# Decoder layer: the feed-forward half as one stage, with 16 bit integers between its parts

## The chip, the cores and the metric

The kernel runs on one core of a Trainium2 chip. The metric is the device time of one execution in microseconds; the time of a kernel is the median of its runs.

## The reference

`x` has 16 sequences of 512 rows of 512 numbers. The first half (attention with a decaying sum, a second scan over the context, two layer norms) gives the rows that the program calls x2. The second half, the one that is changed, is a feed-forward layer with quantized activations and weights, and a last layer norm:

```python
def act_qdq(x):
    scale = jnp.maximum(jnp.max(jnp.abs(x)) / qmax, 1e-12)      # qmax = 32767, one scale for the whole array
    return jnp.clip(jnp.round(x / scale), -qmax - 1.0, qmax) * scale
...
x = act_qdq(x)                                  # (8192, 512)
up = act_qdq(x @ lpbq_dequant(w_up).T)          # (8192, 1536)
gate = act_qdq(x @ lpbq_dequant(w_gate).T)      # (8192, 1536)
sig = fixed_qdq_u16(jax.nn.sigmoid(gate))       # rounded to 16 bit
gate = act_qdq(gate * sig)
o = act_qdq(gate * up)
return o @ lpbq_dequant(w_down).T
```

Each `act_qdq` needs the largest magnitude of its whole array before one element of it can be rounded. So the second half can't run in one pass: s_x, s_u, s_g, s_gs and s_o, the five scales, each close a pass or are found by a shortcut.

## The kernel before

Four engines compute: PE multiplies matrices, DVE and ACT work on tiles of 128 partitions, POOL helps; SP issues DMAs. Every engine runs its own list in the order in which it is written, and waits for the others by counting semaphores. There is no scheduler: the code's order is the engine's order. NB = 16 steps (sequences); T = 512 columns.

A number with 16 bits is multiplied as a sum of two parts, high and low (qh and ql, later oh and ol), with weights that are split in the same way, so one product of 128 x 128 by 128 x 512 takes three matmuls: high by high, low by high weights, high by low weights. A "tile" below is 12 matmuls (four slices of 128 rows, three each) into one PSUM bank; a "chunk" is four tiles, 128 x 2048.

*up_gate_phase.* For each step PE makes 24 tiles, up and gate chunks in turn, into six banks. ACT takes each tile out to `group` (L951) and applies silu to gate chunks (L958). DVE finds maxima of each chunk (L1001, L1004, L1005), and the maximum of silu(gate)·up by chunk (L1008, L1011). SP stores every chunk as 32 bit numbers (L909). The x2 rows of the next step are rounded by DVE (L988), turned by PE in four groups of four transposes (L1054; two groups behind tile 11, two behind tile 13), and split by ACT (L941) and DVE (L993):

```python
if g == 2 and nxt:
    high(b + 1, 1 - par)     # ACT, behind the eviction of tiles 8 to 11
...
if g == 3 and nxt:
    low(b + 1, 1 - par)      # DVE, ahead of the maxima of tiles 12 to 15
```

*scales_phase.* From the maxima s_u and s_g follow. s_gs is taken from the largest gate alone, when silu of it is over 0.28. For s_o only the two chunks with the largest maxima are read again, if the third largest is below the first by more than a margin; otherwise all 48 chunks are passed through twice. The flag `go_through` says which (L1299), and every engine reads it.

*down_phase.* Each chunk of gate and up is read again and goes through POOL (rounding gate and up, L1485, L1490, with a tiny operation ahead of it, L1484), ACT (sigmoid L1515, rounding L1519 and L1524, high part L1531) and DVE (L1558 rounds the sigmoid, L1560 gate by sigmoid, L1566 by up, L1570 the low part). PE multiplies a chunk by the down weights with 48 matmuls (L1616 to L1618). DVE adds the x2 rows (L1578), takes moments (L1581) and `row_moments`, POOL the root (L1494), ACT scales (L1536) and stores. `step` of DVE takes the begin of one chunk, the middle of the one before and the finish of the one before that.

## Time and profile before

| | us |
|---|---|
| median of 3 runs | 3091.08 |
| runs | 3089.62 to 3091.11 |
| span of the profiled execution | 3087.7 |
| median less span | 3.4 |
| first matmul of up_gate_phase | 1294.47 |
| last matmul of up_gate_phase starts | 2369.45 |
| first matmul of down_phase | 2460.56 |
| last matmul of down_phase starts | 3075.71 |

The span runs from the first to the last instruction of the profiled execution; the profile gives no other time of that execution, so the 3.4 us between the median and the span stand for what lies around the span. Matmul records overlap: a record lasts 0.39 us, while the next one starts 0.23 us later. So PE's pace is read from starts.

### The profile page before, as it was taken

How to read it: one execution, taken by the hardware profiler on the slowest of the kernel's cores; microseconds unless marked ns; L12 is line 12 of the kernel's file. 1: busy time of each engine (PE TensorE's matmuls, PEld its weight loads, DVE VectorE, ACT ScalarE, POOL GpSimd, SP SyncE). 2: the span in 40 equal slices, each digit the busy share in tenths (PEclk: the TensorE clock that was granted, in tenths of full speed). 3: DMA queues.
4: the chain of work that ended last, by engine and by line, in shares of the span. 5: the costliest groups of instructions: out<-in, count | busy, mean ns of one | idle time of the engine just before them, and what ended most of it. 6: DMA issues, size and time to landing. Idle time of an engine off the chain costs nothing. (4 is left out here: it accounts for less than half of the span.)

```text
span 3087.7 us, 32437 instructions
## 1 busy us (share of the span) xinstructions
PE 2757.5 (89%) x12272; PEld 2261.6 (73%) x12272; DVE 2280.7 (74%) x2242; ACT 1327.2 (43%) x1396; POOL 588.0 (19%) x266
## 2 busy tenths in 40 slices
PE   2589999999999999599999999999997198988988
PEld 2477777777777777488888888888885177777776
DVE  8678988889888998565555555555555688888886
ACT  2233433444333433243333333333333466666664
POOL 4111111112111111000000000000000485555552
PEclk7789999999999999899999999999998599999999
DMA  6211111111111111332222322222223555555552
GB/s 238 96 41 62 68 54 54 68 60 69 54 54 63 66 54 42 124 140 104 109 109 109 122 109 109 109 102 104 107 109 135 207 205 216 217 217 217 216 206 82
DMA packets 58129, 357.18 MB, mean 116 GB/s; under 512 B 6496, under 2 KB 6496, under 8 KB 17248
## 3 DMA queue, kind: packets, MB, share of 16 engines
q1 hardware_dynamic: 54480, 330.33, 28.5%
q10 hardware_dynamic: 3600, 26.22, 2.1%
q8 instruction: 29, 0.48, 0.1%
q14 instruction: 20, 0.16, 0.0%
HBM read 212.87 MB, written 143.65 MB: 115 GB/s over the span
## 5 line engine op out<-in xcount | busy, mean ns | idle before, releaser
L1062 PE MATMUL ug_out<-ug_qh,ug_wh 128*128 128x512 f32 x1536 | 601.3, 391 | 2.8 <-DVE ug_ql L993 1.4
L1064 PE MATMUL ug_out<-ug_qh,ug_wl 128*128 128x512 f32 x1536 | 598.5, 390 | 0.0
L1063 PE MATMUL ug_out<-ug_ql,ug_wh 128*128 128x512 f32 x1536 | 598.1, 389 | 0.0
L951 ACT ACTIVATE ug_group<-ug_out,scales 128x512 f32<-128x512 f32 x384 | 263.2, 690 | 607.3 <-PE ug_out L1064 604.5
L1616 PE MATMUL dn_ps<-down_wh,dn_oh 128*128 128x512 f32 x768 | 314.4, 409 | 148.3 <-DVE dn_ol L1570 148.3
L1004 DVE TENSOR_REDUCE ug_step_max<-ug_group 128x1 f32<-128x2048 f32 x48 | 109.7, 2285 | 335.4 <-ACT ug_group L951 335.4
L1062 PEld LDWEIGHTS ug_out<-ug_qh,ug_wh 128*128 128x128 f32 x1536 | 288.8, 188 | 62.6 <-DVE ug_wl L1016 2.0
L1064 PEld LDWEIGHTS ug_out<-ug_qh,ug_wl 128*128 128x128 f32 x1536 | 288.6, 188 | 60.5
L1063 PEld LDWEIGHTS ug_out<-ug_ql,ug_wh 128*128 128x128 f32 x1536 | 288.9, 188 | 59.0
L1617 PE MATMUL dn_ps<-down_wl,dn_oh 128*128 128x512 f32 x768 | 310.6, 404 | 0.0
L1618 PE MATMUL dn_ps<-down_wh,dn_ol 128*128 128x512 f32 x768 | 310.2, 404 | 0.0
L1616 PEld LDWEIGHTS dn_ps<-down_wh,dn_oh 128*128 128x128 f32 x768 | 151.8, 198 | 187.3 <-DVE dn_ol L1570 155.1
L717 PE MATMUL qk_ps<-xh,wah 128*128 128x512 f32 x512 | 201.4, 393 | 26.8 <-DVE xl L531 26.8
L1198 POOL MEMSET sc_magic<- 128x1 f32 x1 | 0.1, 99 | 1094.0 <-POOLq L849 1094.0
L718 PE MATMUL qk_ps<-xl,wah 128*128 128x512 f32 x512 | 200.7, 392 | 0.0
L721 PE MATMUL qk_ps<-xh,wal 128*128 128x512 f32 x512 | 200.6, 392 | 0.0
L449 ACT ACTIVATE phi<-qk_ps 128x1024 f32<-128x1024 f32 x64 | 65.9, 1029 | 263.6 <-PE qk_ps L721 263.6
L1001 DVE TENSOR_REDUCE ug_step_max<-ug_group 128x1 f32<-128x2048 f32 x48 | 109.7, 2286 | 90.3 <-ACT ug_group L951 90.3
L1617 PEld LDWEIGHTS dn_ps<-down_wl,dn_oh 128*128 128x128 f32 x768 | 152.3, 198 | 32.2
L1618 PEld LDWEIGHTS dn_ps<-down_wh,dn_ol 128*128 128x128 f32 x768 | 151.4, 197 | 33.0
L1485 POOL TENSOR_SCALAR dn_gate<-dn_gate,scales 128x2048 f32<-128x2048 f32 x48 | 168.6, 3512 | 0.0
L1515 ACT ACTIVATE dn_gs<-dn_gate,scales 128x2048 f32<-128x2048 int16 x48 | 96.6, 2013 | 152.3 <-POOL dn_gate L1485 152.3
(211 smaller groups left out, 5712.6 us busy)
## 6 DMA issues: line engine op xcount, KB each, us to landing
up_products<-ug_group SPq DMA_DIRECT2D x48, 1024.0 KB, 3.9
gate_products<-ug_group SPq DMA_DIRECT2D x48, 1024.0 KB, 3.9
dn_gate<-gate_products SPq DMA_DIRECT2D x48, 1024.0 KB, 4.9
dn_up<-up_products SPq DMA_DIRECT2D x48, 1024.0 KB, 4.8
xt_raw<-in_xT SPq DMA_DIRECT2D x64, 256.0 KB, 2.8
csq<-in_ctx_rows SPq DMA_DIRECT2D x16, 1024.0 KB, 6.7
xrow<-in_x_rows SPq DMA_DIRECT2D x16, 1024.0 KB, 4.8
x_rows<-xrow SPq DMA_DIRECT2D x16, 1024.0 KB, 3.9
```

Of the source, the lines that this page charges most:

```text
L717: pe.matmul(out, sh, mh, start=(k == 0), stop=False)
L718: pe.matmul(out, sh, ml, start=False, stop=False)
L721: mm = pe.matmul(out, sl_, mh, start=False, stop=(k == n - 1))
L951: act.activation(group[:, n % 4, m * T:(m + 1) * T], out_ps[(g * GM + m) % 6][:], ACT.Copy, scale=s_x).then_inc(evacuated, 1)
L1001: dve.tensor_reduce(step_max[:, 0, q:q + 1], part, AX.X, ALU.max, apply_absolute_value=True).then_inc(step_max_ready, 1)
L1062: pe.matmul(o, wh[:, m, k], qh[:, par, k], start=(k == 0), stop=False)
L1063: pe.matmul(o, wh[:, m, k], ql[:, par, k], start=False, stop=False)
L1064: mm = pe.matmul(o, wl[:, m, k], qh[:, par, k], start=False, stop=(k == KC - 1))
L1485: pool.tensor_scalar(gate[:, n], gate[:, n], inv_g, MAGIC, ALU.mult, ALU.add).then_inc(g_round, 1)
L1616: pe.matmul(o, oh[:, n, k, rows], mh, start=(n == 0 and k == 0), stop=False)
L1617: pe.matmul(o, oh[:, n, k, rows], ml, start=False, stop=False)
L1618: mm = pe.matmul(o, ol[:, n, k, rows], mh, start=False, stop=(n == NC3 - 1 and k == KC - 1))
```

## The change

The three phases become one, `ffn_phase`, in one block without barriers inside it. It has three stages. The gate stage makes all gate tiles (12 a step) and stores them as 32 bit numbers, together with the rounded and turned x2 as 16 bit integers. The up stage reads those integers again (no turning), makes all up tiles, and beside them finishes gate chunks: ACT rounds a stored gate chunk to int16 (`gate_chunk_16`) and takes its sigmoid, POOL rounds that to uint16 (`round_sigmoid`), DVE multiplies both and rounds to int16 (`gated`), and SP stores the result. DVE multiplies gs by up for the maxima by tile (192 cells in place of 48 chunks). The down stage reads up as 32 bit and gs as 16 bit numbers; POOL rounds up, DVE makes the rounded product in one instruction (`product`) and the low part, ACT the high part. The weights of one of the three matrices are in SBUF at a time, so they are split again at the start of each stage. Inside the up stage DVE runs `low` of the next step at the head of its round for the third chunk.

```diff
-def up_gate_phase(nc, x2_dram, w_ffn_t, up_dram, gate_dram, amax_x2, acc, rmax, scales):
...
+def ffn_phase(nc, x2_dram, w_ffn_t, q_dram, up_dram, gate_dram, gs_dram, amax_x2, out):
...
+        x2 = raw
+        up16, o16, x2_res = g16, sr16, group
+        banks = [ctx.enter_context(nc.psum_tensor(f"ff_ps{i}", [P, T], F32)) for i in range(8)]
+        turn_ps, out_ps = banks[0:2], banks[2:8]
...
+                def up_step(b, par, ahead):
+                    if ahead:
+                        load_q(b + 1, 1 - par, 16 * (NB // 2))
+                    for g in range(NG):
+                        t = NG * b + g
+                        if ahead:
+                            sp.wait_ge(sr_ready, t + 1)
+                            load_gate(b + 1, g)
+                        sp.wait_ge(gs_ready, t + 1)
+                        sp.dma_start(gs_dram[b, g], gs16[:, g]).then_inc(gs_stored[g], 16)
+                        sp.wait_ge(evacuated, GM * (NG * (NB + b) + g + 1))
+                        sp.dma_start(up_dram[t], group[:, g]).then_inc(stored[g], 16)
...
+                def round_sigmoid(b, par, g, first=False):
+                    t = NG * b + g
+                    pool.wait_ge(sig_ready, t + 1)
+                    if not (first and g < 2):
+                        pool.wait_ge(gs_ready, t - 1)
+                    wait(pool, tick_done, t)
+                    pool.tensor_tensor(tick[:], mhalf[:, 0:1], mhalf[:, 0:1], ALU.mult).then_inc(tick_done, 1)
+                    pool.tensor_scalar(sr16[:, (NG * par + g) % 2], raw[:, g], 65536.0, 0.0, ALU.mult, ALU.add).then_inc(sr_ready, 1)
+
+                def up_step(b, par, ahead):
+                    for g in range(NG):
+                        if g < NG - 1:
+                            round_sigmoid(b, par, g + 1, isinstance(b, int) and b == 0)
+                        elif ahead:
+                            round_sigmoid(b + 1, 1 - par, 0)
...
+                def quantize(b, par):
+                    for c in range(KC):
+                        act.wait_ge(turned, KC * b + c + 1)
+                        if c == 0 and not (isinstance(b, int) and b < 2):
+                            act.wait_ge(q_stored[par], 16 * (b // 2) if isinstance(b, int) else 16 * ((b - par) >> 1))
+                        act.activation(q16[:, par, c], turn_ps[c % 2][:], ACT.Copy, scale=inv_x).then_inc(q_ready, 1)
+                        act.wait_ge(q_ready, KC * b + c + 1)
+                        act.activation(hi[:, par, c], q16[:, par, c], ACT.Copy).then_inc(hi_ready, 1)
...
+                def gate_step(b, par, ahead, first=False):
+                    for g in range(NG):
+                        if not first:
+                            act.wait_ge(stored[g], 16 * b)
+                            act.wait_ge(gate_max_ready, 2 * (NG * (b - 1) + g) + 2)
+                        evacuate(b, par, g, range(GM))
+                        if first and g < NG - 1:
+                            weights_high(g + 1)
+                        if g == 1 and ahead:
+                            quantize(b + 1, 1 - par)
...
+                        evacuate(NB + b, par, g, (0, 1))
+                        if more:
+                            gate_chunk_16(nb, npar, ng, first and ng > 0)
+                        evacuate(NB + b, par, g, (2,))
+                        if more:
+                            gate_chunk_sigmoid(nb, npar, ng)
+                        evacuate(NB + b, par, g, (3,))
+                        if first and g < NG - 1:
+                            weights_high(NG + g + 1)
+                        if not ahead:
+                            weights_high(2 * NG + g)
+                        if g == 1 and ahead:
+                            high(b + 1, 1 - par)
...
+                def low(s, par):
+                    for c in range(KC):
+                        dve.wait_ge(hi_ready, KC * s + c + 1)
+                        dve.tensor_tensor(lo[:, par, c], q16[:, par, c], hi[:, par, c].bitcast(F32),
+                                          ALU.subtract).then_inc(lo_ready, 1)
+
+                def gate_step(b, par, ahead, first=False):
+                    for g in range(NG):
+                        t = NG * b + g
+                        if g == 2 and ahead:
+                            low(b + 1, 1 - par)
+                        if first and g > 0:
+                            weights_low(g)
+                        dve.wait_ge(evacuated, GM * (t + 1))
+                        dve.tensor_reduce(gate_max[:, 0, bass.ds(t, 1)], group[:, g], AX.X, ALU.max).then_inc(gate_max_ready, 1)
+                        dve.tensor_reduce(gate_max[:, 1, bass.ds(t, 1)], group[:, g], AX.X, ALU.min, negate=True).then_inc(gate_max_ready, 1)
+
+                def gated(b, par, g):
+                    t = NG * b + g
+                    sl = (NG * par + g) % 2
+                    dve.wait_ge(sr_ready, t + 1)
+                    if not (isinstance(b, int) and b == 0):
+                        dve.wait_ge(gs_stored[g], 16 * b)
+                    dve.scalar_tensor_tensor(gs16[:, g], sr16[:, sl], gs_factor, g16[:, sl], ALU.mult, ALU.mult).then_inc(gs_ready, 1)
+
+                def up_step(b, par, ahead, first=False):
+                    for g in range(NG):
+                        t = NG * b + g
+                        nb, npar, ng = (b, par, g + 1) if g < NG - 1 else (b + 1, 1 - par, 0)
+                        if g == 2 and ahead:
+                            low(NB + b + 1, 1 - par)
+                        if first and g > 0:
+                            weights_low(NG + g)
+                        dve.wait_ge(evacuated, GM * (NG * (NB + b) + g + 1))
+                        dve.tensor_reduce(up_max[:, bass.ds(t, 1)], group[:, g], AX.X, ALU.max,
+                                          apply_absolute_value=True).then_inc(up_max_ready, 1)
+                        dve.wait_ge(gs_ready, t + 1)
+                        dve.tensor_tensor(prod[:, 0], gs16[:, g], group[:, g], ALU.mult).then_inc(prod_ready, 1)
+                        dve.wait_ge(prod_ready, t + 1)
+                        dve.tensor_reduce(cell_max[:, bass.ds(GM * t, GM)], prod[:, 0].rearrange("p (m t) -> p m t", t=T), AX.X,
+                                          ALU.max, apply_absolute_value=True).then_inc(cell_ready, 1)
+                        if g < NG - 1 or ahead:
+                            gated(nb, npar, ng)
+                        if not ahead and g < NG - 1:
...
+                weights_low(NG)
+                low(NB, 0)
+                dve.wait_ge(gate_top_known, 1)
...
+                dve.wait_ge(cell_ready, NCH)
+                dve.tensor_copy(packed[:, 1:], cell_max[:]).then_inc(packed_ready, 1)
...
+                def product(b, par, g):
+                    t = NG * b + g
+                    sl = (NG * par + g) % 2
...
+                    dve.scalar_tensor_tensor(o16[:, sl].bitcast(I16), gs16[:, g], o_factor, up16[:, sl],
+                                             ALU.mult, ALU.mult).then_inc(o16_ready, 1)
...
+                def down_step(b, par, k=None, bias=True, ahead=True):
+
+                    product(b, par, 1)
+                    ol_chunk(b, par, 0)
+                    if k is not None and bias:
+                        norm_bias(b - 2)
+                    product(b, par, 2)
+                    ol_chunk(b, par, 1)
+                    if k is not None:
+                        sums(b - 1, 1 - par, k)
+                    if ahead:
+                        product(b + 1, 1 - par, 0)
+                    ol_chunk(b, par, 2)
...
+                def turn(b, par, tiles):
+                    pe.wait_ge(x2_in[par], 16 * (b // 2 + 1) if isinstance(b, int) else 16 * ((b - par) >> 1) + 16)
+                    for c in tiles:
+                        wait(pe, q_ready, KC * b + c - 1)
+                        for j in range(TT):
+                            mm = pe.transpose(turn_ps[c % 2][:, j * P:(j + 1) * P],
+                                              x2[:, par, j * HID + c * P:j * HID + (c + 1) * P], ident[:])
+                        mm.then_inc(turned, 1)
+
+                def tile(s, par, m, first):
+                    if not (first and m < 6):
+                        pe.wait_ge(evacuated, MT * s + m - 5)
+                    for k in range(KC):
+                        o = out_ps[m % 6][:]
+                        pe.matmul(o, wh[:, m, k], hi[:, par, k], start=(k == 0), stop=False)
+                        pe.matmul(o, wh[:, m, k], lo[:, par, k], start=False, stop=False)
+                        mm = pe.matmul(o, wl[:, m, k], hi[:, par, k], start=False, stop=(k == KC - 1))
+                    mm.then_inc(out_ready, 1)
+
+                def step(s, par, turn_next=False, weights=None, first=False):
+                    pe.wait_ge(lo_ready, KC * (s + 1))
+                    for m in range(MT):
+                        if weights is not None and m % GM == 0:
+                            pe.wait_ge(wl_ready, weights + m // GM + 1)
+                        tile(s, par, m, first)
+                        if m == 5 and turn_next:
+                            turn(s + 1, 1 - par, (0, 1))
+                        if m == 7 and turn_next:
+                            turn(s + 1, 1 - par, (2, 3))
...
```

ACT's list in a step of the gate stage. Before, in up_gate_phase, behind tile 11 of a step (ug_out are the PSUM banks of tiles, ug_turn those of turned x2):

```order
L951 ACTIVATE ug_group<-ug_out4,scales 128x512
L951 ACTIVATE ug_group<-ug_out5,scales 128x512
L941 ACTIVATE ug_qh<-ug_turn0 128x512
L941 ACTIVATE ug_qh<-ug_turn1 128x512
L941 ACTIVATE ug_qh<-ug_turn0 128x512
L941 ACTIVATE ug_qh<-ug_turn1 128x512
L951 ACTIVATE ug_group<-ug_out0,scales 128x512
```

The same place of the change, behind tile 7 (ff_ps2 and ff_ps3 hold tiles 6 and 7, ff_ps0 and ff_ps1 the turned x2):

```order
L1201 ACTIVATE ff_group<-ff_ps2,ff_scales 128x512
L1201 ACTIVATE ff_group<-ff_ps3,ff_scales 128x512
L1188 ACTIVATE ff_q16<-ff_ps0,ff_scales 128x512
L1190 ACTIVATE ff_hi<-ff_q16 128x512
L1188 ACTIVATE ff_q16<-ff_ps1,ff_scales 128x512
L1190 ACTIVATE ff_hi<-ff_q16 128x512
L1188 ACTIVATE ff_q16<-ff_ps0,ff_scales 128x512
L1190 ACTIVATE ff_hi<-ff_q16 128x512
L1188 ACTIVATE ff_q16<-ff_ps1,ff_scales 128x512
L1190 ACTIVATE ff_hi<-ff_q16 128x512
L1201 ACTIVATE ff_group<-ff_ps4,ff_scales 128x512
```

Each group of turned columns now takes two instructions, the second of which waits for the first, and PE's third and fourth group of transposes, which are behind tile 7 in its list, wait for the first and the second L1188.

DVE's list in a step of the up stage, in the loop, between the second and the third chunk of a step (ff_lo is the low part of the next step's x2, ISA and REGISTER_ALU are waits and their arithmetic):

```order
L1377 TENSOR_REDUCE ff_cell_max<-ff_prod 128x4
L1358 REGISTER_ALU
L1361 SCALAR_TENSOR_TENSOR ff_gs16<-ff_sr16,ff_scales,ff_g16 128x2048
L1340 ISA
L1341 TENSOR_TENSOR ff_lo<-ff_q16,ff_hi 128x512
L1340 REGISTER_ALU
L1341 TENSOR_TENSOR ff_lo<-ff_q16,ff_hi 128x512
L1340 REGISTER_ALU
L1341 TENSOR_TENSOR ff_lo<-ff_q16,ff_hi 128x512
L1340 REGISTER_ALU
L1341 TENSOR_TENSOR ff_lo<-ff_q16,ff_hi 128x512
L1371 ISA
```

Before, the same subtraction (L993) was in the middle of a step of 24 tiles, with 12 tiles to go; now it is behind the four operations of the second chunk, in a step of 12 tiles. In up_gate_phase DVE's list there was:

```order
L1001 TENSOR_REDUCE ug_step_max<-ug_group 128x1
L992 ISA
L993 TENSOR_TENSOR ug_ql<-ug_turn0,ug_qh 128x512
L992 REGISTER_ALU
L993 TENSOR_TENSOR ug_ql<-ug_turn1,ug_qh 128x512
L992 REGISTER_ALU
L993 TENSOR_TENSOR ug_ql<-ug_turn0,ug_qh 128x512
L992 REGISTER_ALU
L993 TENSOR_TENSOR ug_ql<-ug_turn1,ug_qh 128x512
L999 ISA
L1004 TENSOR_REDUCE ug_step_max<-ug_group 128x1
```

The two lists differ in what is ahead of the subtractions (one reduction, against two reductions and two operations on 2048 columns for each chunk) and in their first operand, which is in SBUF now and was in PSUM before.

## Rows read from the trace of the kernel before

**Rows 1.** The page, the granted clock in 40 slices of the span.

```profile
PEclk7789999999999999899999999999998599999999
```

**Rows 2.** Windows of the profile: length, busy time and count by engine, PEclk, DMA share, GB/s.

```profile
1294.50:2370.20 1075.70, 1073.95 (x4848) 890.71 (x4848) 598.19 (x331) 391.55 (x497) 0.00 (x0) 1.00 0.28 111
...
2460.50:3076.50 616.00, 557.93 (x2304) 453.86 (x2304) 524.13 (x401) 404.00 (x242) 340.61 (x148) 0.94 0.55 201
```

**Rows 3.** Timeline of PE: start, duration, and idle time before it in brackets.

```profile
1294.47 0.79 PE L1062 MATMUL ug_out<-ug_qh,ug_wh 128*128 128x512 f32 x1 [1.41 <-DVE ug_ql L993]
...
2369.45 0.39 PE L1064 MATMUL ug_out<-ug_qh,ug_wl 128*128 128x512 f32 x1
...
2460.56 0.80 PE L1616 MATMUL dn_ps<-down_wh,dn_oh 128*128 128x512 f32 x1 [90.72 <-DVE dn_ol L1570]
...
3069.82 0.39 PE L1616 MATMUL dn_ps<-down_wh,dn_oh 128*128 128x512 f32 x1
...
3075.71 0.39 PE L1618 MATMUL dn_ps<-down_wh,dn_ol 128*128 128x512 f32 x1
```

**Rows 4.** Groups by line from 1150 us on: busy us, mean ns, idle before.

```profile
L1485 POOL TENSOR_SCALAR dn_gate<-dn_gate,scales 128x2048 f32<-128x2048 f32 x48 | 168.6, 3512 | 0.0
...
L1570 DVE TENSOR_TENSOR dn_ol<-dn_up,dn_oh 128x2048 fp32r<-128x2048 int16 x48 | 130.2, 2713 | 3.4 <-ACT dn_oh L1531 3.4
...
L1515 ACT ACTIVATE dn_gs<-dn_gate,scales 128x2048 f32<-128x2048 int16 x48 | 96.6, 2013 | 152.3 <-POOL dn_gate L1485 152.3
...
L1578 DVE SCALAR_TENSOR_TENSOR dn_x<-dn_ps,scales,dn_x 128x512 f32<-128x512 f32 x64 | 47.1, 736 | 17.0 <-PE dn_ps L1618 17.0
```

**Rows 5.** Timeline of ACT and DVE at the end of a chunk, in the loop.

```profile
1801.03 1.08 ACT L941 ACTIVATE ug_qh<-ug_turn 128x512 fp32r<-128x512 int16 x2
...
1813.14 0.69 ACT L951 ACTIVATE ug_group<-ug_out,scales 128x512 f32<-128x512 f32 x1 [2.03 <-PE ug_out L1064]
...
1813.86 2.29 DVE L1004 TENSOR_REDUCE ug_step_max<-ug_group 128x1 f32<-128x2048 f32 x1 [4.72 <-ACT ug_group L951]
...
1818.26 2.28 DVE L1008 TENSOR_TENSOR ug_silu<-ug_silu,ug_group 128x2048 f32<-128x2048 f32 x1
...
1820.67 2.29 DVE L1011 TENSOR_REDUCE rmax<-ug_silu 128x2048 f32 x1
```

**Rows 6.** Timeline of PE at a set of transposes.

```profile
2209.18 1.04 PE L1054 MATMUL ug_turn<-ug_ident,ug_x 128*128 128x128 f32 x8
...
2209.97 0.47 PE L1062 MATMUL ug_out<-ug_qh,ug_wh 128*128 128x512 f32 x1
```

**Rows 7.** Timeline of DVE, four subtractions back to back.

```profile
1240.59 2.49 DVE L646 TENSOR_TENSOR al<-att,ah 128x512 fp32r<-128x512 f32 x4
```

**Rows 8.** Timeline of PE: three restarts after idle time.

```profile
608.98 0.50 PE L717 MATMUL mix_ps<-ah,wah 128*128 128x512 f32 x1 [1.42 <-DVE att L612]
...
2640.89 0.50 PE L1616 MATMUL dn_ps<-down_wh,dn_oh 128*128 128x512 f32 x1 [3.12 <-DVE dn_ol L1570]
...
2679.95 0.80 PE L1616 MATMUL dn_ps<-down_wh,dn_oh 128*128 128x512 f32 x1 [4.52 <-DVE dn_ol L1570]
```

**Rows 9.** Timeline of POOL and DVE: the scan with and without POOL, a rounding alone.

```profile
1043.14 5.17 POOL L421 TENSOR_TENSOR csq_l<-csq,csq_h 128x2048 fp32r<-128x2048 f32 x1 [19.15 <-ACT csq_h L480]
...
1043.76 5.63 DVE L551 TENSOR_TENSOR_SCAN kv<-decay,kv 128x512 f32<-128x512 f32 x1
...
1053.62 1.21 DVE L551 TENSOR_TENSOR_SCAN kv<-decay,kv 128x512 f32<-128x512 f32 x1
...
2747.67 1.99 POOL L1490 TENSOR_SCALAR dn_up<-dn_up,scales 128x2048 f32<-128x2048 f32 x1
```

**Rows 10.** A DVE operation of three operands from SBUF: count, min/median/max ns.

```profile
L617 DVE SCALAR_TENSOR_TENSOR att<-att,v_sb x64: 656/692/694, 194.4 to 1240.0; 128x512 f32<-128x512 f32 x64
```

**Rows 11.** Timeline of the decision in the second stage, and SP's first load behind it.

```profile
2384.66 0.15 DVE L1299 CAST sc_go_through<-sc_tmp 128x1 int32<-128x1 f32 x1
...
2387.46 0.36 SPq L1175 DMA_DIRECT2D sc_gate<-gate_products  x1
```

1118 lines of the change are left out of this document (501 added, 617 removed).

## The prediction

> **What bounds the kernel now.** I read the page first, then windows by stage, then PE's timeline at the seams, and last the groups by line. The page's clock row shows the granted clock at its upper level of 2.4 GHz except at the start and at two places, slice 17 (1235 to 1312 us) and slices 31 and 32 (2316 to 2470) [rows 1]: these are the seams between phases. The windows say what is between them. While up and gate tiles are made PE is busy all the time, 1073.95 of 1075.70 us, with DVE at 598 and ACT at 392: that stage is PE's [rows 2]. Then PE stands still for 90.7 us, while the scales are found and the down stage fills [rows 2, 3]. In the down stage DVE is busy for 524 of 616 us and PE has gaps; it runs 16 steps in 615 us, 39 us a step on average [rows 2, 3]. PE's own pace: 26 matmuls apart are 3069.82 and 3075.71, 0.2266 us each [rows 3], so a step of 144 matmuls is 32.63 us, and the down stage has 16 x 6 us to give. The first half, up to 1294.47, is not touched.
>
> **The change part by part.** The sum is made against the profiled span, 3087.7 us; the median of the runs is 3.4 us above it, and I add those back.
>
> *Products.* 4608 matmuls at 0.2266 are 1044.2 us; the window of 1075.7 less this leaves 31.5 us for 15 sets of turning, 2.1 each. The change makes the same matmuls and as many transposes (they don't turn again in the up stage). Nothing is gained or lost here, if PE never waits. It now waits at four kinds of places.
>
> *Gate stage, turning.* PE's third group of transposes, behind tile 7, waits for the first L1188, and ACT has that one behind the eviction of tile 7. Count from the end E of tile 7: eviction E+0.04, next ACT instruction 0.58 later (the spacing of L951, and L941 pairs of 0.60 in 1.08), 0.69 long, so E+1.31; PE's third group at E+1.4. The second L1188 is behind L1190, which waits for its own engine: it ends near E+2.5, PE's fourth group starts at E+2.6 [rows 5]. Half a set takes 0.4 us, so the next tile starts at E+3.05; before, a whole set of eight took 0.79 and the next tile started 0.6 behind E [rows 6]. Loss 2.4 us a step, in 14 steps: **+34**. From below this could be 1.5 a step (both groups wait for one instruction only), from above 2.4 + 1.75 where the clock falls too. It shouldn't: the gaps are 1.3 and 0.7 us, and after 1.42 us of idle the first matmul lasted 0.50, not the 0.80 of a restart at 1.2 GHz [rows 8].
>
> *First gate step.* The low weights of tiles 4 to 7 and 8 to 11 are made by DVE behind the two maxima of the chunk ahead. From a chunk's end: 0.7 for the eviction, 4.5 for two reductions of 2.29, 2.2 for the subtraction: PE waits 7.6 us for the second chunk. For the third there are four subtractions of the next x2 as well (2.5 us, [rows 7]): 9.7. After idle time PE starts at the lower clock. The price of that: 2640.89 to 2679.95 are 39.06 us, of which 4.52 idle and 32.8 work, which leaves 1.75 us, after an idle time of 3.12 [rows 8]; I take 2.2 behind longer ones. Together **+22**. The start itself is 1.5 us earlier, since x2 is turned before the scale is known: **-1.5**.
>
> *Gate to up.* Behind the last gate tile: eviction 0.7, two maxima 4.5, two tiny ones, low weights 2.2, four subtractions 2.4: PE waits 10.4 us. Its next four tiles end near 23; their chunk's maximum, product, cell maxima and `gated` (2.29 each, 8.9 in all, [rows 5]) stand ahead of the next low weights: 12.2 more. For the third chunk the same and four subtractions: 14.5. With three restarts of 2.2: **+44**. Before, this seam did not exist.
>
> *Up stage, steady.* DVE has 3 x 8.9 + 2.5 = 29.3 us of work in a step of 32.63, ACT 23, POOL 6 to 11, by 2.0 us for a rounding alone and its mean of 3.5 where DVE's operations stand in its way [rows 4, 9]. So PE should set the pace, but the order is tight. Count from S, PE's first matmul of a step. Tile 7 ends at S+21.9, its eviction at S+22.7, DVE starts the maximum 0.03 later [rows 5]. Then 2.2 (next), 2.2 and 0.2 for the wait on its own result (1818.26 to 1820.67 is 2.41), 2.2, 2.2: the subtractions start at S+31.7, 0.60 apart, and the last ends at S+34.2 [rows 5, 7]. PE wants it at S+32.63. Loss 1.6 us a step, and at such an idle time the clock stays. It holds for 14 steps (the first up step has its successor ready early): **+22**.
>
> *Up to down.* Behind the last up tile: eviction 0.7, maximum, product and cell maxima 6.8, the reduction over partitions of 193 columns 1.3, some ten small DVE operations 2: the flag at 11. SP's first load came 2.8 us behind the flag [rows 11]; I estimate that two pairs of small loads land at 18, then ACT 1.1, DVE 2.4, the last low weights 2.3, the scale 1, POOL's first rounding 2 to 4, and `product` 2.3 twice, low part 2.3: PE starts 35 us behind its last tile, where it was 90.7 [rows 3]: **-56**. Bounds: 28 with every load ahead, 50 if the loads or POOL's rounding wait for each other.
>
> *Down stage.* DVE: three times `product` and low part, 4.6 us (the low part's mean of 2.71 has POOL's interference in it), and the sums, 4 x 1.4 + 0.8: 20 us of 32.63. ACT: 3 x 2.0 + 3. POOL 6.5 to 12 [rows 4]. The low part of the third chunk is ready some 4 us ahead of its use. Loads of the next step wait for the store of two steps before and land, by my estimate, 8 us into the step; `product` wants them at 10.5. So PE sets the pace: 16 x 32.63 + 2 against 615.4: **-91**. From above +30 if those loads are late by 2 us in each step. The tail is unchanged.
>
> Sum: 34 + 22 - 1.5 + 44 + 22 - 56 - 91 = -26.5. 3087.7 - 26.5 + 3.4 = 3064.6; I forecast **3065 us**.
>
> *A rule against it.* `gated` is a scalar_tensor_tensor with both tensors in SBUF, and neither is bfloat16. The nearest row is L617, 692 ns for 512 columns, what any two-input operation takes [rows 10]; so I price 2048 columns at 2.29. The Trainium skill, Vector Engine (DVE) Microarchitecture Reference, section "Points that are easy to get wrong", says that such an instruction runs at half rate. This case's trace disagrees, with 692 ns; by the rule it would be 1.3 us for 512 columns, and the total is that of the last rival below.
>
> **The rivals.**
>
> *POOL takes DVE's place in the up stage (slower).* ACT's sigmoid of the next step's first chunk starts at S+30.7 and lasts 2.01 [rows 4], so POOL's small operation comes at S+32.8 to 32.9 and its rounding 0.2 later, while DVE is in its four subtractions (S+31.7 to 34.2). The rows of the first half show who wins. POOL's L421 came at 1043.14 behind a DVE operation; the scan that DVE had next lasted 5.63 in place of 1.21: POOL got in at the boundary, and DVE stood still until it was through [rows 9]. Here a rounding that gets in ahead of the fourth subtraction holds it for the 2.0 us that it lasts alone [rows 9]. PE then waits 3.5 us, and at 3.12 to 3.5 the clock falls (1.75, above): 5.2 a step in place of 1.6, 14 x 3.6 = 51 more, 3065 + 51 = **3115**. It turns on 0.1 us: POOL's small operation must be there before the third subtraction starts, at S+32.9. Each DVE operation that is a little longer than I take it (an integer operand, a scale from SBUF) speaks for it, each wait of ACT or POOL against it. Which instructions wait for POOL can't be read off before, where only DVE operations with two SBUF inputs did; the maxima aren't among them, I take them as free. Chance 0.30. The GPSIMD Engine Reference of the Trainium skill, section "Specifications", names the same two engines' shared SBUF interfaces; the trace agrees, with those 5.63 us.
>
> *The down stage doesn't get PE's pace.* If the late loads or POOL hold the third chunk, 37 us a step, +70: 3135 with the rest as forecast; at 34 a step it is +22, 3087. Against it: DVE's and ACT's load halves. Chance 0.10.
>
> *The change doesn't shorten the search for s_o.* If the condition for all chunks held, 96 passes over a chunk of some 10 us each: over 4000. The reference's numbers for these inputs give 42500 for the largest cell and 38719 for the third, against a margin of 4.9. Chance below 0.01.
>
> *Waits that I price are hidden.* If DVE's chain is 1 us shorter and the seams half as long: -45 more, **3020**. Chance 0.08.
>
> *`gated` at half rate.* DVE then has 35.7 us in a step, PE waits 3.7 and restarts slowly: 14 x 3.8 = 53 more, 3118, and some 35 on top where POOL also gets in. By L617 chance 0.05.
>
> **How the numbers follow.** My own case has 0.46; its range is 3045 to 3085 (10 either way at both long seams, 0.9 a step in turning). The range of 3040 to 3125 takes in POOL's rival, which may also hold in only some of the steps. Slower by over 0.2% (6 us, what a measurement of this kernel can tell): POOL's rival in most steps, half the down rival, half rate, a little of my case's errors: 0.32. Within: 0.08. Faster: 0.60.
>
> **What the new profile would show.** PE's idle time ahead of the third and fourth group of transposes, 0.7 to 1.3 us, 15 times. The first matmul of an up step waiting for DVE's last subtraction, 1.5 us (right) or 3.5 with a slow restart (POOL's rival; then that subtraction lasts 2.6 us and not 0.68). PE's longest idle time near 35 us. Down steps of 32.7 us with the clock at 1.00. Wrong it would be by a wait that I read as slack: ACT's evictions behind its two long operations, or loads in the down stage.

## The result, and the profile after

The changed kernel takes 3137.0 us (median of 4 runs, 3136.1 to 3137.9) against 3091.1 us of the kernel before beside it (3089.6 to 3091.6). The ratio is 1.0148, with a 95% interval of 1.0134 to 1.0163: slower by 46 us. The forecast was 3065 us, faster, with a range of 3040 to 3125. It was wrong in sign, and the time lies outside the range.

The profiled execution has a span of 3136.0 us, 48.3 us more than before. First the page's row of the granted clock, which answers to [rows 1].

```profile
PEclk7689999999999999799999998899999978999999
```

Then the windows by stage of the changed kernel: first half, gate stage, the seam with 110 of the first up step's 144 matmuls, the rest of the up stage, the wait between up and down, the down stage, the tail. Columns are as in [rows 2].

```profile
0.00:1294.92 1294.92, 1128.23 (x5121) 918.78 (x5121) 1093.09 (x1441) 483.74 (x633) 217.75 (x99) 0.95 0.20 74
1294.92:1911.41 616.49, 573.08 (x2544) 468.07 (x2544) 251.09 (x156) 211.67 (x318) 0.00 (x0) 0.97 0.32 123
1911.41:1980.00 68.59, 31.79 (x110) 25.04 (x111) 38.23 (x35) 24.80 (x23) 8.48 (x7) 0.70 0.47 184
1980.00:2553.19 573.19, 526.02 (x2196) 428.14 (x2194) 465.38 (x238) 328.62 (x331) 100.72 (x90) 0.95 0.57 216
2553.19:2599.17 45.98, 0.00 (x1) 0.03 (x1) 24.07 (x27) 7.56 (x5) 12.07 (x9) 0.53 0.68 251
2599.17:3123.98 524.81, 524.81 (x2304) 433.98 (x2304) 317.52 (x309) 132.31 (x106) 191.84 (x106) 1.00 0.48 191
3123.98:3136.00 12.02, 0.00 (x1) 0.00 (x0) 2.24 (x8) 2.93 (x4) 1.01 (x1) 0.60 0.21 87
```

The down stage is what the change promised: PE is busy for all of 524.81 us at clock 1.00, where the same 2304 matmuls had 615.44 us before. What eats this, and more, lies in the two product stages. Before, they were one window of 1075.7 us with PE busy throughout [rows 2]. Now they are three, of 616.49 + 68.59 + 573.19 = 1258.27 us, and in none of them is PE always busy. PE's timeline says where it stands; these rows are its restarts (the first matmul behind an idle time), and the bracket is the idle time ahead of each.

```profile
1316.05 0.80 PE L1577 MATMUL ff_ps<-ff_hi,ff_wh 128*128 128x512 f32 x1 [7.49 <-DVE ff_wl L1335]
...
1340.74 0.79 PE L1577 MATMUL ff_ps<-ff_hi,ff_wh 128*128 128x512 f32 x1 [4.95 <-DVE ff_wl L1335]
...
1921.65 0.80 PE L1577 MATMUL ff_ps<-ff_hi,ff_wh 128*128 128x512 f32 x1 [10.24 <-DVE ff_lo L1341]
...
1946.36 0.79 PE L1577 MATMUL ff_ps<-ff_hi,ff_wh 128*128 128x512 f32 x1 [12.08 <-DVE ff_wl L1335]
...
1974.72 0.79 PE L1577 MATMUL ff_ps<-ff_hi,ff_wh 128*128 128x512 f32 x1 [14.49 <-DVE ff_wl L1335]
...
2176.60 0.49 PE L1577 MATMUL ff_ps<-ff_hi,ff_wh 128*128 128x512 f32 x1 [3.37 <-DVE ff_lo L1341]
...
2599.17 0.77 PE L1617 MATMUL ff_ps<-ff_wh,ff_hi 128*128 128x512 f32 x1 [45.98 <-DVE ff_lo L1511]
```

The row at 2176.60 stands for 14 alike, one at each up step from the third on, all of 3.37 us. In the gate stage the transposes wait twice a step, 1.36 and 0.58 us in 12 of its 15 sets (1.45 and 0.52 in two, 3.25 and 0.52 in the first).

The same numbers as a balance against the kernel before, where 2304 matmuls at 0.2266 us are 522.1 us and the 15 sets of turning 31.5 us:

| part | forecast | measured | from |
|---|---|---|---|
| start of the second half | -1.5 | +0.5 | 1294.92 against 1294.47 |
| gate stage: turning and first step | 34 + 22 = 56 | +62.9 | 616.49 - 522.1 - 31.5 |
| gate to up, and up steps | 44 + 22 = 66 | +119.7 | 68.59 + 573.19 - 522.1 |
| up to down | -56 | -44.7 | 45.98 against 90.72 |
| down stage | -91 | -90.6 | 524.81 against 615.44 |
| sum | -26.5 | +47.8 | |

The rest to 48.3 is the tail and rounding. The up part alone is 54 us off. Split further: the three waits at the seam are 36.8 us, with 7.1 us of matmuls at the lower clock, 43.9 together (44 was forecast). So the 14 steady steps lose 75.8 us in place of 22: 47.2 of idle time and 28.6 of matmuls that follow each other more slowly behind it, for the most part at the lower clock (e1 shows how much).

What happens at one of these 14 is in the timelines of DVE and POOL.

```profile
2172.28 4.18 DVE L1341 TENSOR_TENSOR ff_lo<-ff_q,ff_hi 128x512 fp32r<-128x512 int16 x4
...
2174.09 2.37 DVE L1341 TENSOR_TENSOR ff_lo<-ff_q,ff_hi 128x512 fp32r<-128x512 int16 x1
...
2173.36 0.27 POOL L1121 TENSOR_TENSOR ff_tick<-ff_mhalf 128x1 f32<-128x1 f32 x1 [8.96 <-ACT ff_raw L1225]
2173.59 2.34 POOL L1122 TENSOR_SCALAR ff_sr<-ff_raw 128x2048 uint16<-128x2048 f32 x1
```

The first DVE row is the group of four subtractions; the second shows its last one alone. It starts at 2174.09, lasts 2.37 us where its sisters last 0.68, and ends 0.5 us behind POOL's rounding, which began at 2173.59, 0.1 us after the third had started. That looks like the collision that the first half showed with the scan [rows 9]. But an overlap is only an overlap: DVE's chain was late by itself too. The experiments take the two apart.

### The profile page after: what moved, and what is told of

Read it like the earlier page. It is cut to its first block, busy times and chain, and to the rows that moved or that the text cites. A ratio compares the mean times of both kernels' runs of the same rounds, so it can differ in the third digit from the quotient of the medians.

```text
span 3136.0 us, 33437 instructions
## 1 busy us (share of the span) xinstructions
PE 2783.9 (89%) x12272; PEld 2274.0 (73%) x12272; DVE 2191.6 (70%) x2213; ACT 1191.6 (38%) x1420; POOL 531.9 (17%) x311
## 3 DMA queue, kind: packets, MB, share of 16 engines
q1 hardware_dynamic: 72912, 394.04, 32.9%
## 4 chain that ended last, share of the span: by engine, by line
PE 46%; DVE 8%; issue 3%; ACT 2%; POOL 0%; DVEq 0%; POOLq 0%; ACTq 0%
PE ff_ps L1577 10%; PE ff_ps L1578 10%; PE ff_ps L1579 10%; PE ff_ps L1617 5%; PE ff_ps L1618 5%; PE ff_ps L1619 5%; DVE ff_lo L1341 2%; DVE ff_up_max L1372 1%; DVE ff_gs L1361 1%; DVE ff_prod L1375 1%; PE ff_ps L1568 1%; ACT ff_q L1188 1%; DVE ff_wl L1335 0%; ACT ff_group L1201 0%; DVE ff_cell_max L1377 0%
## 5 line engine op out<-in xcount | busy, mean ns | idle before, releaser
L1577 PE MATMUL ff_ps<-ff_hi,ff_wh 128*128 128x512 f32 x1536 | 622.7, 405 | 99.2 <-DVE ff_lo L1341 60.2
L1578 PE MATMUL ff_ps<-ff_lo,ff_wh 128*128 128x512 f32 x1536 | 615.3, 401 | 0.0
L1579 PE MATMUL ff_ps<-ff_hi,ff_wl 128*128 128x512 f32 x1536 | 613.8, 400 | 0.0
L1201 ACT ACTIVATE ff_group<-ff_ps,ff_scales 128x512 f32<-128x512 f32 x384 | 264.8, 690 | 683.2 <-PE ff_ps L1579 670.2
L1577 PEld LDWEIGHTS ff_ps<-ff_hi,ff_wh 128*128 128x128 f32 x1536 | 299.9, 195 | 170.2 <-issue 53.0
L1579 PEld LDWEIGHTS ff_ps<-ff_hi,ff_wl 128*128 128x128 f32 x1536 | 298.9, 195 | 64.7
L1578 PEld LDWEIGHTS ff_ps<-ff_lo,ff_wh 128*128 128x128 f32 x1536 | 300.3, 195 | 62.1
L1617 PE MATMUL ff_ps<-ff_wh,ff_hi 128*128 128x512 f32 x768 | 299.9, 390 | 46.0 <-DVE ff_lo L1511 46.0
L1618 PE MATMUL ff_ps<-ff_wl,ff_hi 128*128 128x512 f32 x768 | 299.7, 390 | 0.0
L1619 PE MATMUL ff_ps<-ff_wh,ff_lo 128*128 128x512 f32 x768 | 299.5, 390 | 0.0
```

The costliest lines, as they stand in the source:

```text
L1201: act.activation(group[:, g, m * T:(m + 1) * T], out_ps[(GM * g + m) % 6][:], ACT.Copy, scale=s_x).then_inc(evacuated, 1)
L1577: pe.matmul(o, wh[:, m, k], hi[:, par, k], start=(k == 0), stop=False)
L1578: pe.matmul(o, wh[:, m, k], lo[:, par, k], start=False, stop=False)
L1579: mm = pe.matmul(o, wl[:, m, k], hi[:, par, k], start=False, stop=(k == KC - 1))
L1617: pe.matmul(o, hi[:, sl, k, rows], mh, start=(g == 0 and k == 0), stop=False)
L1618: pe.matmul(o, hi[:, sl, k, rows], ml, start=False, stop=False)
```

## The experiments

Two theories of the 46 us stood against each other. **Collision**: POOL's rounding takes the place of the last subtraction, and PE's wait grows beyond what the clock bears. **Order**: DVE's chain of long operations is simply too long ahead of the subtractions, and POOL only runs beside it. Seven kernels were run, each made from the changed kernel; e6 and e7 carry several of the changes. Added lines shift line numbers by up to six. The code shown is an excerpt of each change; ... stands for lines left out.

**e1, POOL waits.** POOL's rounding for the next step stays behind the four subtractions; no work moves on DVE.

```
                         elif ahead:
+                            pool.wait_ge(lo_ready, KC * (NB + b + 2))
                             round_sigmoid(b + 1, 1 - par, 0)
```

> In the up stage POOL's rounding of the next step's first sigmoid chunk waits until DVE's four subtractions are through; nothing else is changed. Theory A (POOL gets in ahead of the fourth subtraction and holds DVE): the four subtractions last 2.5 us in place of 4.18, PE's first matmul of an up step waits 1.6 us in place of 3.37, 14 times, which is 25 us. Whether the clock still falls at 1.6 us is open: if it stays, another 26 us come back (75.8 of the steady stage less 47.2 idle is 28.6) and the kernel takes 3086 us; if it falls as before, 3112 us. Theory B (the wait is DVE's own chain of three 2048-column operations a chunk, which are longer than priced, and POOL only runs beside it): the wait stays 3.37 us and the time 3137 us.

Measured: 3088.8 us (10 runs, 3086.4 to 3091.5), 48 us below the changed kernel and level with the kernel before (ratio 0.999, 0.9981 to 1.0). One step of e1, in the timelines of DVE, POOL and PE:

```profile
2156.70 2.49 DVE L1342 TENSOR_TENSOR ff_lo<-ff_q,ff_hi 128x512 fp32r<-128x512 int16 x4
...
2159.67 1.90 POOL L1122 TENSOR_SCALAR ff_sr<-ff_raw 128x2048 uint16<-128x2048 f32 x1
...
2159.33 0.49 PE L1578 MATMUL ff_ps<-ff_hi,ff_wh 128*128 128x512 f32 x1 [1.68 <-DVE ff_lo L1342]
2159.66 0.40 PE L1579 MATMUL ff_ps<-ff_lo,ff_wh 128*128 128x512 f32 x1
```

The four subtractions last 2.49 us, the wait is 1.68 us at all 14 steps, and steps are 34.60 us apart in place of 37.6 to 39.2. The window over them shows the second half of the gain:

```profile
1984.65:2470.72 486.07, 462.58 (x2025) 378.68 (x2024) 413.48 (x225) 305.77 (x310) 86.16 (x84) 1.00 0.66 246
```

PE's clock is 1.00 there (0.95 in the changed kernel). Of the 48 us, 14 x 1.69 = 24 are idle time and the other 24 are the clock. A step is still 34.60 us, 32.63 of work, 1.68 of waiting and 0.29 at the restart, so some 4 of the 28.6 us above belong to the restarts even at the upper clock. The expectation of theory A was 3086 us. The collision theory is shown, with its size, by one wait that takes POOL away and nothing else. What DVE's order costs by itself is the 1.68 us of waiting that stay: close to the 1.6 of the forecast.

**e2, low parts early.** The other way to the same end: POOL is left alone, and DVE makes the subtractions two operations earlier.

```
-                        if g == 2 and ahead:
-                            low(NB + b + 1, 1 - par)
...
                         dve.tensor_tensor(prod[:, 0], gs16[:, g], group[:, g], ALU.mult).then_inc(prod_ready, 1)
+                        if g == 1 and ahead:
+                            low(NB + b + 1, 1 - par)
```

> In the up stage the four subtractions of the next step's integers move ahead in DVE's order by two operations: behind the product of the second chunk, ahead of its cell maxima and of the next gate chunk's product. No work is removed and POOL's instructions are as they were. They would end 4.6 us earlier in the step, 3 us ahead of PE's need, and POOL's rounding would meet other DVE operations that nothing waits for. Theories A (POOL's hold) and B (DVE's own chain) both give no wait at the start of an up step, 47 us of idle and 28 us of slow clock back: 3061 us, up steps of 32.7 us. Theory C (DVE, ACT and POOL are too full for a step of 32.63 us, so that the wait comes back in another place, at the evictions or the products): 3100 us or more.

Measured: 3061.7 us (3059.3 to 3063.5), ratio to the kernel before 0.9904 (0.9887 to 0.992). 75 us come back, the 75.8 that the steady steps lost. The up steps of e2 in one window:

```profile
1983.60:2476.19 492.59, 492.59 (x2174) 407.54 (x2172) 440.42 (x238) 325.63 (x329) 108.28 (x90) 1.00 0.67 251
```

PE has no idle time in 492.59 us, with DVE at 440. So DVE was never too full for the stage; moving four operations up in its list is enough, with POOL's list as it was. Theory C, that the wait would come back elsewhere, falls. This run can't tell collision from order, since both expected its result; e1 does that. POOL's rounding now meets other operations, and one such place is instructive:

```profile
2181.41 2.34 DVE L1361 SCALAR_TENSOR_TENSOR ff_gs<-ff_sr,ff_scales,ff_g 128x2048 int16<-128x2048 uint16 x1
...
2182.55 1.25 POOL L1121 TENSOR_TENSOR ff_tick<-ff_mhalf 128x1 f32<-128x1 f32 x1 [8.97 <-ACT ff_raw L1225]
```

Here POOL's small operation came in the middle of a long DVE operation, and it was POOL that stood still: 1.25 us in place of 0.19 (e1), until DVE's 2.34 us were over. POOL's rounding then ran from 2183.77 on beside the maximum, which has one input and was not held:

```profile
2183.67 2.28 DVE L1370 TENSOR_REDUCE ff_up_max<-ff_group 128x2048 f32 x1
```

**e3, turning split.** ACT takes the first two turned tiles between the evictions of tiles 5 and 6.

```
-                        evacuate(b, par, g, range(GM))
+                        if g == 1 and ahead:
+                            evacuate(b, par, g, (0, 1))
+                            quantize(b + 1, 1 - par, (0, 1))
+                            evacuate(b, par, g, (2, 3))
+                            quantize(b + 1, 1 - par, (2, 3))
+                        else:
+                            evacuate(b, par, g, range(GM))
...
-                        if g == 1 and ahead:
-                            quantize(b + 1, 1 - par)
```

> In the gate stage ACT takes the first two turned tiles between the evictions of tiles 5 and 6 and the last two behind that of tile 7, so that PE's third and fourth group of transposes find their banks free. The two waits of 1.36 and 0.58 us go in 14 steps (27 us), and 3.8 us in the first step. Theory A (the clock falls in every other gate step because of these two small gaps; such steps last 38.4 us against 36.8): another 11 us, together 3095 us, gate steps of 34.7 us. Theory B (the transposes themselves lower the clock, as they show 0.63 us for four): the 11 us stay, 3106 us.

Measured: 3092.5 us (10 runs, 3090.3 to 3094.4), 44.5 us below the changed kernel, ratio to the kernel before 1.0003 (0.9994 to 1.0013). The gate stage of e3:

```profile
1293.00:1866.81 573.81, 557.29 (x2544) 462.15 (x2544) 250.97 (x156) 211.68 (x318) 0.00 (x0) 0.98 0.34 132
```

It lasts 573.81 us against 616.49. Of the 42.7 us, 26.9 are idle time (43.4 less the 16.5 that remain in the first step) and 15.8 are matmuls at the lower clock and transposes that are no longer cut in two. The time is 2.5 us below theory A's: with the same transposes and no gaps the clock stays at 1.00 from 1377 to 1860 us, where the changed kernel has 0.98, so theory B falls. Small gaps cost the clock as well, and the two of 1.36 and 0.58 us, with four transposes between them, did lower it, though 1.68 us alone in e1 did not. In the first step nothing was gained: the 3.25 us wait went, and the wait for low weights behind it grew from 4.95 to 9.02 us.

**e4, seams.** Low weights ahead of the maxima, high weights ahead of the evictions, and all three groups of up weights during and just behind the last gate step. This is DVE's part; ACT's high weights and SP's loads of weights move with it.

```
-                        if first and g > 0:
-                            weights_low(g)
+                        if first and g < NG - 1:
+                            weights_low(g + 1)
                         dve.wait_ge(evacuated, GM * (t + 1))
...
+                        if not ahead and g < 2:
+                            weights_low(NG + g)
+                            if g == 1:
+                                low(NB, 0)
...
-                        if first and g > 0:
-                            weights_low(NG + g)
...
-                weights_low(NG)
-                low(NB, 0)
+                weights_low(NG + 2)
```

> Low weights come ahead of the maxima in DVE's order and high weights ahead of the evictions in ACT's at both places where weights change: in the first gate step, and between gate and up, where all three groups of up weights and the first subtractions are made while the last gate step runs and just behind it. If DVE's order is all that makes these five waits (7.49 and 4.95; 10.24, 12.08 and 14.49 us), they go with their restarts at the slow clock: 36.8 + 7.1 at the seam, some 12.4 + 4 in the first gate step, 60 us together, 3077 us. Rival: the transfers of the weights (a buffer for two of them) or the search for the gate scale, which ACT and POOL wait for with all evictions behind it, take their place: half of it at most, 3105 us.

Measured: 3090.2 us (10 runs, 3086.8 to 3093.2), 47 us below the changed kernel, between the two expectations. All five waits for weights are gone, and one new wait stands at the second up step. In the timeline of PE, and behind it of POOL and DVE:

```profile
1938.37 0.80 PE L1579 MATMUL ff_ps<-ff_hi,ff_wh 128*128 128x512 f32 x1 [12.49 <-DVE ff_lo L1342]
...
1898.93 2.32 POOL L1114 PARTITION_ALL_REDUCE ff_gate_top_all<-ff_gate_top  x1 [611.32 <-DVE ff_gate_top L1401]
1911.73 0.18 POOL L1122 TENSOR_TENSOR ff_tick<-ff_mhalf 128x1 f32<-128x1 f32 x1 [10.48 <-issue]
...
1913.91 4.05 DVE L1366 SCALAR_TENSOR_TENSOR ff_gs<-ff_sr,ff_scales,ff_g 128x2048 int16<-128x2048 uint16 x1 [10.34 <-POOL ff_sr L1123]
```

PE now goes through the first up step without a stop, but `gated` for the first chunk can't be made until the gate scale is known and POOL has rounded. DVE begins its chunks of 9.0 us at 1913.9, and the subtractions of the second step stand behind them. The wait moved from the weights to the scale; 12.5 us of idle and a restart are the price. Of POOL's 10.48 us, the last 4.5 are behind the sigmoid that it needed (ready at 1907.2): POOL was not ready itself.

**e5, rounding first.** This looks at up to down, where the wait was 46 us and not 35. In the changed kernel:

```profile
2577.07 2.31 POOL L1160 PARTITION_ALL_REDUCE ff_amax_o<-ff_amax_o  x1 [11.36 <-DVE ff_amax_o L1488]
2588.17 0.18 POOL L1152 TENSOR_TENSOR ff_tick<-ff_mhalf 128x1 f32<-128x1 f32 x1 [8.79 <-issue]
...
2590.45 4.11 DVE L1505 SCALAR_TENSOR_TENSOR ff_sr<-ff_gs,ff_scales,ff_g 128x2048 int16<-128x2048 int16 x1 [10.10 <-POOL ff_g L1153]
```

The scale was known at 2580.3, and DVE then waited 10.1 us for POOL, which stood still for 8.8 us behind its reduction and waited for no other engine.

```
+                round_up(0, 0, 0, True)
+                round_up(0, 0, 1, True)
                 pool.wait_ge(o_max_part, 1)
                 pool.partition_all_reduce(amax_o[:], amax_o[:], P, bass.bass_isa.ReduceOp.max).then_inc(o_reduced, 1)
-                round_up(0, 0, 0, True)
-                round_up(0, 0, 1, True)
                 round_up(0, 0, 2, True)
```

> Between up and down POOL rounds the first two chunks of up products ahead of its reduction over partitions of the largest product, and not behind it; their data and scale are there by then. In the changed kernel POOL's first small operation starts 8.8 us behind the end of that reduction though nothing it needs is late. Theory A (POOL needs these 9 us for its first ordinary operation behind any such reduction): with the roundings ahead of it they are done when the scale s_o is known, DVE's first product starts at once behind the scale instead of 10.1 us later, and PE's wait between up and down falls from 46 to 36 to 38 us, a gain of 8 to 10 us, 3128 us. Theory B (POOL waits for something that the trace does not name, such as the loads of up products): its roundings start at the same time as before, the reduction itself is delayed behind them, and the kernel gains nothing or loses some us.

Measured: 3130.0 us (3129.8 to 3130.5), 7 us below the changed kernel; its ratio to the kernel before is 1.0121 (1.0104 to 1.0138). PE's wait is 39.8 us, 6.1 less. The timeline of POOL in e5:

```profile
2571.55 0.18 POOL L1152 TENSOR_TENSOR ff_tick<-ff_mhalf 128x1 f32<-128x1 f32 x1 [7.14 <-issue]
2571.73 1.96 POOL L1153 TENSOR_SCALAR ff_g<-ff_raw,ff_scales 128x2048 int16<-128x2048 f32 x1
...
2583.36 0.38 POOL L1162 PARTITION_ALL_REDUCE ff_amax_o<-ff_amax_o  x1 [6.59 <-issue]
2593.45 0.18 POOL L1152 TENSOR_TENSOR ff_tick<-ff_mhalf 128x1 f32<-128x1 f32 x1 [9.72 <-issue]
```

DVE's first product follows the scale at once, as theory A said. But POOL paid at the other side too: the reduction, whose input was there at 2576.0, started only at 2583.36, 6.6 us behind POOL's last rounding, and the next rounding 9.7 us behind the reduction. The wait of 7.14 us in the first row comes on top: a memset, at 2564.31, lies between it and the reduction before. The timeline leaves out one kind of row that names what all these pauses have in common. The views of single lines have it (changed kernel, then e5):

```profile
L1138 POOLq MODIFY_POOL_CONFIG  x2: 6/6/6, 2545.6 to 2545.6; - x2
L1152 POOLq MODIFY_POOL_CONFIG  x2: 83/83/83, 2579.3 to 2579.4; - x2
...
L1152 POOLq MODIFY_POOL_CONFIG  x4: 11/46/83, 2564.4 to 2583.7; - x4
L1162 POOLq MODIFY_POOL_CONFIG  x2: 8/8/8, 2577.0 to 2577.0; - x2
```

In every run a pair of these small instructions stands on POOL's queue at the start of each of these pauses, in both directions. Where POOL goes on at once, as from the first reduction to the `affine_select` behind it at 1287.44, there is none, nor ahead of the memset that comes 2.9 us behind a reduction. Where POOL had to wait anyway the pause is hidden: the pair of L1138 stands at 2545.6, right behind the last rounding, and its reduction starts at 2561.78, 0.1 us behind its input. In e5 the pair of L1162 makes the pause ahead of the reduction: the scale is known 8.7 us behind the reduction's input, where it took 3.4 in the changed kernel. These 5.3 us are why PE's wait fell by 6.1 us and not by the 10.1 of DVE's. What POOL does between the pair and the next operation the rows don't say. The Trainium skill, GPSIMD Engine Reference, section "Instruction dispatch", says that the first call to freshly loaded code costs about 6 us, with nothing visible in the profile for that time, and measures it from the instruction of this name. That fits; the pauses with nothing else to wait for are 6.0 (e6) to 10.1 us here, and no run took the change of code away.

**e6, together**: e2, e3, e4 and e5.

> The edits of e2, e3, e4 and e5 together. From 3137 us e2 took 75, e3 took 44.5 and e4 took 47. If their waits are independent and e5 takes 9, the time is 2961 us. The 12.5 us wait that e4 left at the second up step shrinks with e2's order by two operations, 4.5 us, so 2957 us. Rival: an up stage that starts with ACT and DVE behind (the evictions of the first up step queue behind the search for the gate scale) does not catch up when PE no longer pauses at each step, and waits come back step by step: 2990 us or more.

Measured: 2958.4 us (2956.1 to 2959.4), ratio to the kernel before 0.9564 (0.9548 to 0.958). The four gains of 75, 44.5, 47 and 7 us add up to 173.5, and 178.6 came: they are all but independent. Of the 5 us more, 2.2 are the wait at the second up step, which is now 10.25 us, and another 2.3 lie in the first gate step, where e3 alone had gained nothing because the low weights came late. In the windows of e6 (gate stage with the first up step; the other 15 up steps; down stage) PE is all but never idle:

```profile
1294.12:1878.63 584.51, 584.50 (x2688) 485.79 (x2688) 277.90 (x183) 235.19 (x342) 8.47 (x7) 1.00 0.38 146
1878.63:2380.38 501.75, 491.50 (x2160) 406.66 (x2160) 455.00 (x247) 328.32 (x331) 109.33 (x90) 0.99 0.67 254
2419.70:2944.63 524.93, 524.93 (x2304) 434.23 (x2304) 318.59 (x309) 132.31 (x106) 190.25 (x107) 1.00 0.48 192
```

What is left beside PE's own work in the second half is one wait of 10.25 us at the second up step and one of 39.3 us between up and down.

**e7, low parts first.** e6, with the high parts and the subtractions of the second up step behind the first chunk. One condition changes in two places, ahead of `low` in DVE's list and ahead of `high` in ACT's:

```
-                        if g == 1 and ahead:
+                        if g == (0 if first else 1) and ahead:
                             low(NB + b + 1, 1 - par)
```

It also builds the identity for the transposes ahead of POOL's first reduction and not behind it.

> e6, and in the first up step ACT makes the high part and DVE the subtractions of the next step's integers behind the first chunk in place of the second. Theory A (PE's wait at the second up step is only for these subtractions, which stand behind four chunks of 8.9 us that began late): that wait goes, 8 us and a slow restart of 2 us below e6, 2947 us. Theory B (the four chunks themselves are late, so PE then waits for the evictions of the second up step): no gain over e6.

Measured: 2957.4 us (2956.4 to 2959.0), the same as e6. PE's waits, in its timeline:

```profile
1881.00 0.50 PE L1583 MATMUL ff_ps<-ff_hi,ff_wh 128*128 128x512 f32 x1 [0.49 <-DVE ff_lo L1346]
...
1921.05 0.79 PE L1583 MATMUL ff_ps<-ff_hi,ff_wh 128*128 128x512 f32 x1 [7.12 <-DVE ff_lo L1346]
```

The wait at the second step fell from 10.25 to 0.49 us, and a new one of 7.12 us stands at the third. So theory A is refuted in what matters: DVE is behind by its chunks, and with 29 us of work in a step of 32.6 it needs more than a step to catch up. From the first product to the last up tile e7 takes 1.7 us less than e6, not 10. The expectation names e6 and one edit; the identity was a second one. POOL's timeline, and behind it PE's last matmul of the first half in e6 and in e7:

```profile
1278.69 0.29 POOL L1110 TENSOR_SCALAR_AFFINE_SELECT ff_ident<-ff_ident 128x128 f32<-128x128 f32 x1 [0.15 <-POOL ff_mhalf L1108]
1289.09 0.38 POOL L1112 PARTITION_ALL_REDUCE amax_x<-amax_x  x1 [10.11 <-issue]
...
1258.01 0.47 PE L717 MATMUL mix_ps<-csq_h,strip_h 128*128 128x512 f32 x1 [0.88 <-DVE xrow L660]
...
1259.27 0.47 PE L717 MATMUL mix_ps<-csq_h,strip_h 128*128 128x512 f32 x1 [0.87 <-DVE xrow L660]
```

PE turned x2 four microseconds earlier than in e6, but POOL's reduction, and with it the scale, came later: the first product starts at 1295.73 us, 1.6 later than in e6 (1294.12). Of these, 1.3 us were there before: the first half, which no edit touches, ended that much later in this execution. Counted from its last matmul the first product comes 36.46 us later in e7 and 36.11 in e6. So the identity gained nothing, and what it cost, 0.35 us, is no more than single executions differ by.

## Why the prediction was wrong

**The step that failed** is the forecast's choice in "Up stage, steady": "the subtractions start at S+31.7, 0.60 apart, and the last ends at S+34.2. [...] Loss 1.6 us a step, and at such an idle time the clock stays." By itself this is right: e1 has 1.68 us and the clock at 1.00. What its sum left out is POOL's hold on DVE, the rival that stood beside it with a chance of 0.30. POOL's small operation came 0.13 us before the third subtraction started (2173.36 and 2173.49, in the step shown; it is so in all 14) and its rounding 0.5 us before the fourth, and it came out as that rival said: subtractions of 4.18 us, a wait of 3.37 (3.5), 75.8 / 14 = 5.4 us a step (5.2). The term was 22 and measured 75.8; 54 of the 75 us by which the sum missed are here. The text said that it turns on 0.1 us and then took the favourable side. Its own numbers did not support this: POOL's small operation at S+32.8 to 32.9 against the third subtraction's start at S+32.9, with a note that each integer operand or scale that made DVE later spoke for the collision. `gated` measured 2.25 from start to start where 2.2 was taken, and nothing made ACT later. Two events that are 0 to 0.1 us apart by estimate are as likely in the one order as in the other, and a rival that costs 51 us at even odds takes away the whole of a forecast of -26.

**Gate stage, turning.** Waits of 1.36 and 0.58 us for 1.3 and 0.7: right, and so, within 1 us, was the first step (7.49 and 4.95 + 3.25 + 0.52 for 7.6 and 9.7). "It shouldn't [fall]", of the clock, is wrong: it fell in 6 of the 12 steps with gaps of 1.36 and 0.58 us, which last 38.4 us in place of 36.8. The single gap of 1.42 in [rows 8] was the wrong row for two gaps close together. Nor does a first matmul of 0.50 us show by itself that the clock stays: at 2176.60 it lasted 0.49, and the fourth, 0.8 us later, was slow:

```profile
2177.39 0.62 PE L1577 MATMUL ff_ps<-ff_hi,ff_wh 128*128 128x512 f32 x1
```

The stage is 6.9 us above its forecast in the balance; by e3 the clock and the cut transposes are 15.8.

**Gate to up.** 10.24, 12.08 and 14.49 us for 10.4, 12.2 and 14.5, and 7.1 us at the lower clock for 6.6: counting the queue of DVE instruction by instruction gave the whole seam to 0.2 us.

**Up to down.** 46.0 us for 35, inside its bounds of 28 to 50. The term of POOL's first rounding, "2 to 4", is the one that was mis-sized: from the known scale (2580.35) to the rounded chunk (2590.31) it took 10.0 us, because POOL started 8.8 us behind its reduction (e5). The small loads, for which the forecast had no row, landed 2 us later than estimated, and the first `product` took 4.11 us for 2.3.

**Down stage.** -90.6 for -91, no wait of PE in 16 steps; the rival of late loads didn't occur, although loads of up products take 9.3 us.

**Start.** -1.5 was to come from turning x2 ahead of the scale. PE could not turn: the identity for its transposes stood in POOL's list behind the reduction, and that began 9.0 us behind POOL's last operation (9.2 before the change). The +0.5 of the balance is not the change's: the first half ended 1.2 us later in this execution (its last matmul at 1258.89, against 1257.70). Counted from there the start came 0.7 us earlier. This row of the changed kernel is the reduction:

```profile
1287.17 0.38 POOL L1108 PARTITION_ALL_REDUCE amax_x<-amax_x  x1 [9.02 <-issue]
```

**`gated` at half rate.** The rule named in the forecast, from the Trainium skill, Vector Engine (DVE) Microarchitecture Reference, section "Points that are easy to get wrong", would give some 4.6 us for 2048 columns, by estimate. The row shows 2.34 us for two 16 bit inputs, and [rows 10] said the same of float32. Where `gated` lasts 4.05 (e4), POOL's rounding ran beside its first 1.9 us.

## What to carry to other kernels

When a step is moved from one engine's list to a place where another engine has a free moment, compare the absolute times of both engines' long operations at that place, and treat an order that hangs on 0.1 us as open, with the costlier side in the sum. An operation that PE waits for belongs as early in its engine's list as its inputs allow, not where it last was: two places earlier were worth 75 us here, and none of the work had changed. It helps only while the engine isn't behind with all its work: at the second up step of e7 it moved the wait by one step. And a stage that is split in two needs its preparations (weights, scales, the first inputs) moved into the stage before, since every one left behind is paid in full: the five waits at the two seams and their restarts cost 47 us net.

## What the runs showed of the hardware

- POOL and DVE hold each other up, in both directions. A rounding of POOL that begins during a DVE subtraction holds the next one, which then lasts 2.37 us and not 0.68; a small POOL operation that arrives in the middle of a DVE operation waits for its end (1.25 in place of 0.19 us). A maximum with one input that runs beside POOL keeps its 2.28 us. The Trainium skill, GPSIMD Engine Reference, section "Specifications", lists DVE instructions with two SBUF inputs among those that contend with GpSimd; these rows agree.
- The granted clock fell to 0.5 behind each of the 14 idle times of 3.37 us (1.7 us lost each time on average, against the steps of e1), and behind none of the 14 idle times of 1.68 us. It fell in 6 of 12 steps with gaps of 1.36 and 0.58 us that lie 0.7 us of transposes apart, and never with the same transposes and no gaps (e3).
- POOL pauses where it changes between ordinary operations and its reduction over partitions, in both directions, and each pause starts with a pair of MODIFY_POOL_CONFIG. With nothing else to wait for: 7.1 us (e5), 8.8 and 9.7 us from a reduction towards a rounding, 6.0, 6.6, 9.0 and 10.1 us ahead of a reduction. A memset or an `affine_select` behind a reduction has no such pair; they came 2.9 and 0.0 us behind it. A pause that falls into a wait of POOL's costs nothing (16.41 us of waiting, the reduction at 2561.78).
